# First two image pairs convolved from the colour planes, with warm-up products on TensorE

## The reference

```python
w = (0.2989, 0.587, 0.114)
gray = jnp.einsum('bchw,c->bhw', x, w)[:, None]
edges = conv_general_dilated(gray, scharr, window_strides=(1, 1), padding='SAME', ...)
h = jnp.sqrt(jnp.square(edges)).sum(axis=1) / 2
...
k, v, r = (einsum('btc,dc->btd', mix(layernorm(h)), W) for W in (Wk, Wv, Wr))
h = h + einsum('btc,dc->btd', sigmoid(r) * wkv(w, u, k, v), Wo)   # wkv: a scan over 256 tokens
h = h + experts(layernorm(h))    # one of 8 experts per token: gelu((xhat*s+b) @ W1 + b1) @ W2 + b2
```

## Time and profile before

| what | us |
|---|---|
| median of 3 runs | 1179.91 (1176.8 to 1180.4) |
| the profiled execution | 1180.26 |
| its span, first to last instruction | 1178.5 |
| PE busy | 1097.7 (93%) |
| DVE busy | 1033.9 (88%) |
| ACT busy | 880.0 (75%) |
| POOL busy | 171.4 (15%) |

### The profile page before, as it was taken

The page is one execution under the profiler, slowest core; times in us unless marked ns, Lnnn a source line. Parts: engine busy times, 40 slices in busy tenths (PEclk is TensorE's granted clock), DMA queues, the critical chain, the costliest instruction groups (busy, mean ns, idle before and its releaser), DMA issues.

```text
span 1178.5 us, 17076 instructions
## 1 busy us (share of the span) xinstructions
PE 1097.7 (93%) x5699; PEld 715.6 (61%) x5699; DVE 1033.9 (88%) x1869; ACT 880.0 (75%) x1407; POOL 171.4 (15%) x234
## 2 busy tenths in 40 slices
PE   0647899999999999999999999999999999999987
PEld 0223466666666666666666666666666666666665
DVE  2587799999999999999999999999999999999851
ACT  0366687888788878878888878888888788877641
POOL 4021110101111101011111111111111111110000
PEclk9878899999999999999999999999999999999999
DMA  7986667667766776677767676677676766760001
GB/s 190 204 161 110 103 149 158 141 123 153 152 140 135 156 153 146 123 141 155 144 136 146 154 153 134 124 163 148 131 147 146 163 136 123 152 99 22 19 18 36
DMA packets 163601, 155.70 MB, mean 132 GB/s; under 512 B 12444, under 2 KB 163570, under 8 KB 163570
## 3 DMA queue, kind: packets, MB, share of 16 engines
q1 hardware_dynamic: 125972, 119.77, 41.4%
q0 software_dynamic: 32640, 31.46, 21.6%
q10 hardware_dynamic: 4958, 4.07, 1.5%
HBM read 105.96 MB, written 65.03 MB: 145 GB/s over the span
## 4 chain that ended last, share of the span: by engine, by line
PE 88%; DMA 6%; SPq 2%; ACT 1%; DVE 1%; POOL 0%; issue 0%; ACTq 0%; POOLq 0%
PE bank L1135 26%; PE bank L1270 19%; PE bank L1198 15%; PE bank L1125 10%; PE bank L1174 9%; PE bank L1219 4%; DMA gray_dram<-planes 2%; DMA gray_dram<-rows_in 2%; DMA rows_in<-gray_dram 2%; PE bank L1248 2%; PE bank L1271 1%; PE bank L1210 1%; PE bank L1257 1%; SPq L346 1%; PE bank L1186 1%; DMA gray_dram<-in_x_dram 1%
## 5 line engine op out<-in xcount | busy, mean ns | idle before, releaser
L1270 PE MATMUL bank<-w_sb,hidden 128*128 128x256 f32 x1024 | 238.8, 380 | 1.9 <-ACT hidden L963 1.9
L1270 PEld LDWEIGHTS bank<-w_sb,hidden 128*128 128x128 f32 x1024 | 184.8, 191 | 30.1 <-ACT hidden L963 2.6
L1125 PE MATMUL bank<-rows_in,conv_w 102*32 102x512 f32 x1024 | 138.3, 641 | 47.9 <-DMA rows_in<-gray_dram 47.9
L1135 PE MATMUL bank<-mixed_r,w_r_t 128*128 128x512 f32 x256 | 127.4, 622 | 8.8 <-ACT v_sb L892 8.8
L1198 PE MATMUL bank<-normed_hi,w_hi 128*128 128x512 f32 x256 | 128.2, 501 | 3.2 <-DVE normed_lo L721 3.2
L1135 PE MATMUL bank<-mixed_v,w_v_t 128*128 128x512 f32 x256 | 122.0, 600 | 0.4 <-ACT edge L876 0.4
L1174 PE MATMUL bank<-w_o_t,rwkv 128*128 128x256 f32 x512 | 116.9, 382 | 0.3 <-DVE rwkv L695 0.3
L440 POOL TENSOR_TENSOR pool_turn<-pool_turn 128x1 f32<-128x1 f32 x30 | 5.5, 184 | 721.8 <-ACT planes L884 676.3
L1174 PEld LDWEIGHTS bank<-w_o_t,rwkv 128*128 128x128 f32 x512 | 98.2, 192 | 15.7 <-issue 1.1
L1198 PE MATMUL bank<-normed_lo,w_hi 128*128 128x512 f32 x256 | 101.4, 396 | 0.0
L1198 PE MATMUL bank<-normed_hi,w_lo 128*128 128x512 f32 x256 | 100.8, 394 | 0.0
(11 more groups left out here) (144 smaller groups left out, 2308.3 us busy)
## 6 DMA issues: line engine op xcount, KB each, us to landing
rows_in<-gray_dram SPq DMA_DIRECT2D x186, 256.0 KB
planes<-in_x_dram SPq DMA_DIRECT2D x124, 256.0 KB, 3.5
gray_dram<-planes POOLq DMA_DIRECT2D x120, 256.0 KB, 5.9
out_dram<-resid SPq DMA_DIRECT2D x64, 256.0 KB, 2.2
gray_dram<-in_x_dram SPq DMA_DIRECT2D x60, 256.0 KB, 5.1
rows_in<-gray_dram SPq DMA_DIRECT2D x124, 24.0 KB
rows_in<-gray_dram ACTq DMA_DIRECT2D x6, 256.0 KB
planes<-in_x_dram ACTq DMA_DIRECT2D x4, 256.0 KB, 7.3
```

What stands on the lines that cost most here:

```text
L1125: ins = pe.matmul(bank[BANK_EDGE[n]][ROW_TILE * q:ROW_TILE * (q + 1), :], conv_w[0:TAPS, c, :], rows, start=True, stop=True)
L1135: ins = pe.matmul(ps[:, :], weights[:, kt, ct * P:(ct + 1) * P], part[:, 2 * kt:2 * kt + 2, :].rearrange("p i t -> p (i t)"), start=(kt == ...
L1270: pe.matmul(ps, hidden[:, m, i, rows], w2_sb[:, m, :], start=(m == 0), stop=False)
```

## The change

- The first two pairs no longer go through gray. `load_colors` brings, for each pair, the red, green and blue rows straight from `x` into `rows_in`: the three groups of 32 partitions now hold the three colours, unshifted, and the six extra partitions the rows above and below in each colour (zeroed by DVE where there are none). SP and ACT take one image each, first the first pair, then the second.
- `convolve` does three accumulating products for such a pair where there was one: a centre one of 512 columns and two of 2 x 255 columns, displaced by one to the right or left in the result. Their weights `color_w` are built by DVE from the taps, the filter and the gray weights (`shade`).
- PE first runs `WARM_UP = 12` products of a cleared tile of 128 x 512 in fp32, as soon as DVE has cleared it.
- ACT's list has the filter's 18 numbers first, then the rows, then the parameters and Wr, and last the shifted filter taps and the zero borders of `gray_dram`, now written as two strips of lines and 4 x 257 pairs of elements.
- SP's `load_later_weights` stands before step 3 instead of step 2. DVE's `conv_w` and `ident_bf` are built in `setup_first_layer`, before step 3. POOL builds taps first, then the identity; the mask and the clearing of `b2_raw` come last.

The core of the diff:

```diff
+        def load_colors(eng, pair, i):
+
+            buf, base = pair % 2, (2 * pair + i) * NCOL * T * D
+            for color in range(NCOL):
+                src = bass.AP(x.tensor, base + color * T * D, [[D, ROW_TILE], [ROW_TILE * D, TILES], [1, D]])
+                eng.dma_start(rows_in[buf][ROW_TILE * color:ROW_TILE * (color + 1), :, i, :], src
+                              ).then_inc(rows_loaded[buf], 16)
+            if pair < 2:
+                eng.wait_ge(s_outside, 2 * pair + 2)
+            for k in range(2):
+                src = bass.AP(x.tensor, base + (ROW_TILE - 1 + k) * D,
+                              [[T * D, NCOL], [ROW_TILE * D, TILES - 1], [1, D]])
+                first = 3 * ROW_TILE + 3 * k
+                eng.dma_start(rows_in[buf][first:first + 3, 1 - k:TILES - k, i, :], src
+                              ).then_inc(rows_loaded[buf], 16)
...
-            load_first(sp, 0, 0)
-            load_first(sp, 1, 0)
-            store_first(sp, 0, 0)
-            sp.wait_ge(s_borders, 16)
-            sp.wait_ge(first_stored[0], 16 * HALF)
-            load_rows(sp, 0, 0)
-            store_first(sp, 1, 0)
+            load_colors(sp, 0, 0)
+            load_colors(sp, 1, 0)
             for src, dst in zip((Wk, Wv), w_raw):
                 sp.dma_start(dst, src.rearrange("(a p) c -> p a c", p=P)).then_inc(s_w_in, 16)
-            sp.wait_ge(first_stored[1], 16 * HALF)
-            load_rows(sp, 1, 0)
...
+                    if at.is_step(FIRST + GRAY):
+                        sp.wait_ge(s_borders, 32)
...
-            run_steps(sp, step, {2: load_later_weights})
+            run_steps(sp, step, {3: load_later_weights})
...
-            first_gray_of(0)
-            dve.wait_ge(s_scharr_dj_in, 80)
+            for b in range(2):
+                dve.memset(rows_in[b][3 * ROW_TILE:TAPS, 0, :, :], 0.0).then_inc(s_outside, 1)
+                dve.memset(rows_in[b][3 * ROW_TILE:TAPS, TILES - 1, :, :], 0.0).then_inc(s_outside, 1)
+            dve.memset(zeros, 0.0).then_inc(s_zeros, 1)
+            for color in range(NCOL):
+                dve.memset(shade[ROW_TILE * color:ROW_TILE * (color + 1), :], GRAY_WEIGHTS[color])
+            for n in range(6):
+                dve.memset(shade[3 * ROW_TILE:TAPS - n, :], GRAY_WEIGHTS[2 - n % 3]).then_inc(s_shade, 1)
+                dve.wait_ge(s_shade, n + 1)
+
+            dve.wait_ge(s_scharr_all_in, 16)
+            done(dve.tensor_scalar(scharr_all[0:TAPS, :], scharr_all[0:TAPS, :], shade[0:TAPS, :], 0.5,
+                                   ALU.mult, ALU.mult))
             dve.wait_ge(s_cleared, CLEARED_TAPS)
+            for di in range(3):
+                for c in range(2):
+                    weights = scharr_all[0:TAPS, 9 * c + 3 * di:9 * c + 3 * di + 3]
+                    ins = dve.tensor_tensor((color_w if di == 0 else color_part)[0:TAPS, c, :, :],
+                                            taps[0:TAPS, di, :].unsqueeze(1).to_broadcast([TAPS, 3, ROW_TILE]),
+                                            weights.unsqueeze(2).to_broadcast([TAPS, 3, ROW_TILE]), ALU.mult)
+                if di > 0:
+                    ins.then_inc(s_color_part, 1)
+                    dve.wait_ge(s_color_part, di)
+                    done(dve.tensor_tensor(color_w[0:TAPS, :, :, :], color_w[0:TAPS, :, :, :],
+                                           color_part[0:TAPS, :, :, :], ALU.add))
...
             def setup_first_layer():
+                setup_conv()
                 dve.wait_ge(s_w1_in, 32)
...
+            act.wait_ge(s_zeros, 1)
+            act.dma_start(bass.AP(gray_dram.tensor, 0, [[IMAGE, 4], [(T + 1) * PITCH + 1, 2], [1, T + 1]]),
+                          zero_pairs[:, 0:T + 1].unsqueeze(1).to_broadcast([4, 2, T + 1])).then_inc(s_borders, 16)
+            act.dma_start(bass.AP(gray_dram.tensor, D + 1, [[IMAGE, 4], [PITCH, T + 1], [1, 2]]),
+                          zero_pairs.rearrange("p (t k) -> p t k", k=2),
+                          allow_slow_non_contiguous=True).then_inc(s_borders, 16)
...
-            pe.wait_ge(s_dve_setup, SETUP_CONV)
+            pe.wait_ge(s_zeros, 1)
+            for _ in range(WARM_UP):
+                pe.matmul(bank[BANK_Y[1]][:, :], zeros[:, 0:P], zeros[:, 0:512], start=True, stop=True)
+            pe.wait_ge(s_dve_setup, SETUP_FIRST)
...
+                rows = rows_in[at.buf(EDGE)][0:TAPS, 4 * half:4 * half + 4, :, :]
+                if at.has_later(EDGE):
...
+                else:
+                    sums = pair_view(bank[BANK_EDGE[n]])
+                    for dj, to, of in ((1, 0, 0), (0, 1, 0), (2, 0, 1)):
+                        width = D - (dj != 1)
+                        for q in range(4):
+                            ins = pe.matmul(sums[ROW_TILE * q:ROW_TILE * (q + 1), :, to:to + width],
+                                            color_w[0:TAPS, c, dj, :], rows[:, q, :, of:of + width],
+                                            start=(dj == 1), stop=(dj == 2))
```

More of the change, by code:

```diff
@@ L190, in vision_layer @@
         w1_scaled = resid[0][:, :, :].rearrange("p (a b) d -> p a (b d)", a=CH)
[L191 to L195, removed]
+        late_flat = resid[3][:, :, :].rearrange("p b d -> p (b d)")
+        color_w = late_flat[:, 0:6 * ROW_TILE].rearrange("p (c j r) -> p c j r", c=2, j=3)
+        color_part = late_flat[:, 6 * ROW_TILE:12 * ROW_TILE].rearrange("p (c j r) -> p c j r", c=2, j=3)
+        scharr_all = late_flat[:, 12 * ROW_TILE:12 * ROW_TILE + 18]
+        shade = late_flat[:, 12 * ROW_TILE + 18:12 * ROW_TILE + 19]
+        zeros = resid[2][:, :, :].rearrange("p b d -> p (b d)")[:, 0:2 * (T + 1)]
+        zero_pairs = zeros[0:4, :]
         w1_raw = hidden[:, 0:2, :, :].rearrange("p a b c -> p a (b c)")
@@ L210, in vision_layer @@
         planes_in = [sem(f"planes_in{i}") for i in range(2)]
[L211 to L214, removed]
+        s_outside, s_shade, s_zeros, s_scharr_all_in = [sem(n) for n in ("outside", "shade", "zeros", "scharr_all_in")]
+        s_color_part = sem("color_part")
         s_params_in, s_scharr_dj_in, s_borders = sem("params_in"), sem("scharr_dj_in"), sem("borders")
@@ L427, in _ @@
             pool.memset(eps[:, 0:1], LN_EPS)
-            pool.memset(eps[:, 1:2], LN_EPS * LN_EPS)
+            pool.memset(eps[:, 1:2], LN_EPS * LN_EPS).then_inc(s_built, 1)
+            pool.memset(b2_raw, 0.0).then_inc(s_cleared, 1)
+            pool.memset(mask_rows[:, :], MASK_OUT).then_inc(s_cleared, 1)
+            pool.wait_ge(s_cleared, CLEARED_B2 + 1)
+            for g in range(NM):
+                rows = slice(32 * g, 32 * (g + 1))
+                pool.affine_select(out=mask_rows[rows, :], in_=mask_rows[rows, :], compare_op=ALU.is_ge, fill=0.0,
+                                   base=0, pattern=[[1, E * H]], channel_multiplier=-H).then_inc(s_cleared, 1)
+                pool.wait_ge(s_cleared, CLEARED_B2 + 2 + 2 * g)
+                pool.affine_select(out=mask_rows[rows, :], in_=mask_rows[rows, :], compare_op=ALU.is_ge, fill=0.0,
+                                   base=H - 1, pattern=[[-1, E * H]], channel_multiplier=H).then_inc(s_cleared, 1)
+                pool.wait_ge(s_cleared, CLEARED_B2 + 3 + 2 * g)
+            pool.tensor_scalar(mask_rows[:, :], mask_rows[:, :], -1.0, MASK_OUT, ALU.mult, ALU.add
+                               ).then_inc(s_cleared, 1)
             pool.memset(b2_parts[:, :], 0.0)
             pool.memset(wg_t[:, :, :], 0.0)
-            pool.memset(route[:, :, :], 0.0).then_inc(s_built, 1)
+            pool.memset(route[:, :, :], 0.0).then_inc(s_cleared, 1)
             def step(at):
@@ L492, in _ @@
-                done(ins)
-            first_gray_of(1)
-            dve.wait_ge(s_built, 1)
-            done(dve.tensor_copy(ident_bf[:, :], ident[:, :]))
-            assert own[0] == SETUP_CONV
+                    weights = scharr_all[0:TAPS, 9 * c + 3 * di:9 * c + 3 * di + 3]
+                    ins = dve.tensor_tensor((color_w if di == 0 else color_part)[0:TAPS, c, :, :],
+                                            taps[0:TAPS, di, :].unsqueeze(1).to_broadcast([TAPS, 3, ROW_TILE]),
+                                            weights.unsqueeze(2).to_broadcast([TAPS, 3, ROW_TILE]), ALU.mult)
@@ new lines, in _, with setup_conv @@
+                if di > 0:
[3 more added lines that the diff above has]
+                                           color_part[0:TAPS, :, :, :], ALU.add))
+            assert own[0] == SETUP_FIRST
+            def setup_conv():
+                dve.wait_ge(s_scharr_dj_in, 80)
+                done(dve.tensor_scalar(scharr_dj[0:TAPS, :], scharr_dj[0:TAPS, :], 0.5 * GRAY_WEIGHTS[2], None,
+                                       ALU.mult))
+                for di in range(3):
+                    for c in range(2):
+                        weight = scharr_dj[0:TAPS, 3 * c + di:3 * c + di + 1]
+                        if di == 0:
```

(9 more changed lines are left out.)

129 lines of the change are left out of this document (37 added, 92 removed).

## The result

The changed kernel takes 1165.95 us in the median of its runs against 1180.16 of the kernel before beside it; the ratio is 0.988, with a 95% interval of 0.985 to 0.991. The forecast for the time was 1165.3 us. The profiled execution was the longest of the four, at 1167.08 us; its span, from the first to the last instruction, is 1165.3 us and only by chance the same number as the forecast.

What follows compares the result with a forecast made beforehand. PE bounds the loop, so time is the third convolution's start plus 1089.5 us. C at 26.9, scaling's end 46.3 and 28.1 more put that start at 74.4 instead of 89.03: forecast 1165.3 us, range 1160 to 1175.

Steps and rivals of the forecast that it cites:

- The sum: Start of the kernel: added-up terms put the third pair's convolution at 74.4 us, 14.6 earlier than 89.03.
- zeros: PE's start: twelve fp32 products of zeros take 24 x 0.43 + 2.5 = 12.8 us, ending at 16.6.
- first convolution: First pair on PE: 24 groups of 0.43 us make 10.3 us, or 20.5 if the level does not hold.
- C: End of the first pair's convolution: forecast at 26.9 us, 13.1 earlier than the 39.96 before.
- its first two results: Second pair's convolution: 12 groups instead of 4, 12 x 0.43 + 2.5 = 7.7 us, reaching 43.7.
- from there to the third: End of scaling to third convolution: the old 29.1 us stretch stays, less 1.0 for a POOL operation, giving 28.1.
- the POOL operation of 2.06 us: One-element operation at 67.15 before the third convolution: beside a DVE scan, perhaps not in the new order; 1.0 taken off.
- the rival with 0.12: Rows late, chance 0.12: both pairs share the queues, first pair lands at 20 to 22, 4 to 5 us lost, 1170.
- The clock rival: Chance 0.12: zeros may not raise PE's level, or narrow products lose it; C 37.1, gain 4.4, kernel 1175.5 us.
- the planes' early arrival: Step 3: third pair's plane loads, now ahead of the weights, are long in, so scaling ends at 46.3 us.
- The rival with 0.06: ACT held, chance 0.06: short descriptors hold ACT until 37, C counts as 39, gain about 2, kernel 1177.9 us.
- The slack before the first scan of step 4: DVE's idle time there: 5.69 - 4 - 1.6 leaves 0.1 us, so DVE's later work is just hidden.

Runs made afterwards that it cites:

- e2: Changed kernel with 20 products of zeros instead of 12; ratio to the kernel before 0.9952, third convolution 6.0 us later than in the first trace.
- e1: Changed kernel without the products of zeros (WARM_UP = 0); ratio to the kernel before 0.9901, third convolution at 76.27 us.
- e7: Changed kernel without zeros, SP and ACT holding the second pair's row loads until the first pair's rows landed; ratio to the kernel before 0.9879.
- e5: Changed kernel with only the centre product for the first two pairs, so edges differ from the reference; one execution, span 1158.1 us, third convolution 68.27.
- e3: Changed kernel with the experts' weights issued before step 2 on SP again, ahead of the third pair's planes; ratio to the kernel before 0.9888.
- e10b: As e8, but Wk, Wv, parameters and Wr loaded before the second pair's rows, and nine products of zeros; ratio to the kernel before 0.9891.
- e6: Changed kernel with ACT's scaling of the third pair moved ahead of absolute(0) and absolute(1) in step 3; ratio to the kernel before 0.9883.
- e11b: As e10b, with scharr_dj loaded right behind the first pair's rows and setup_conv() called before step 0; ratio to the kernel before 0.9857, median 1162.85 us.
- e8: Changed kernel with the edits of e6 and e7 together and seven products of zeros; ratio to the kernel before 0.9878, median 1162.4 us.
- e4: Kernel before with only the experts' weights moved on SP, issued before step 3 instead of step 2; ratio to the kernel before 0.9997.
- e9b: The changed kernel measured and traced again, unchanged (the repeat); ratio to the kernel before 0.9891, median 1165.51 us.

## Why the prediction was right

**The third convolution.** The sum said 74.4; the trace says 74.35 and, again, 74.40. Its terms, in us:

| term | forecast | first trace | repeat |
|---|---|---|---|
| start of PE | 3.8 | 3.80 | 3.81 |
| zeros | 12.8 | 13.26 | 12.50 |
| first convolution | 10.3 | 10.46 | 10.46 |
| its end, C | 26.9 | 27.5 | 26.8 |
| C to the second convolution | 9.07 | 8.9 | 8.9 |
| its first two results | 7.7 | 7.14 | 8.45 |
| end of scaling | 46.3 | 46.05 | 46.6 |
| from there to the third | 28.1 | 28.3 | 27.8 |

The mechanism is the one forecast, and every term is within 0.8 us. That the sum is right to 0.05 us is luck, for the misses cancel. The start of PE is exact because a memset takes 0.48 to 0.49 us and not 0.6, while the first starts at 0.99 and not at 0.8. In the last stretch the POOL operation of 2.06 us came back almost whole (0.19 at 54.03), where I had taken off 1.0; but from the end of the scaling to the red add it now takes 1.9 us (0.45 of them the operation at 46.20), and had taken 1.1 from the landing of blue.

**That C is on the path** is shown by e2: 6.7 us more in front became 6.0 at the third convolution, and the time rose with it.

**The rows.** I took their landing at 14.5; it is 15.5 (e1). The zeros end 1.5 us later, 0.8 in the repeat, so the miss cost nothing. That the second pair in the queue delays the first, the rival with 0.12, is true, with 2.4 us (e7), and the range of 20 to 22 that I gave it was too dark.

**The zeros.** The sum took them as given and did not price the kernel without them. They are worth 1.9 us of the 14.7 at the third convolution (e1). The rest is by subtraction the new way of the rows, net of the 6.1 us that the tripling costs (e5); no run takes that way back alone. The clock rival did not come: with zero products PE's level rose after 4 to 5.5 us, and in the narrow products that followed it stayed (groups 0.43 us apart up to 26.44). In the sum, 24 x 0.43 + 2.5 = 12.8, the 0.43 is the distance of the zeros' weight loads from 9.61 on (before, mixed_v's eight instructions took 3.60), and for the 2.5 of a start at the low level the two traces show 3.0 and 2.2 (13.26 and 12.50 less 10.3).

**The order on SP.** The prediction gave the planes' early arrival as the reason why scaling would not wait. The planes are early, but e3 shows that they would have been in time in the old order too. The step was right in its sum and wrong in the weight it gave the move.

**ACT.** I put it free at 20 to 24; it was at 22.4 with its table loaded, 5 us before it was needed at C. The rival with 0.06 did not come here, but e10b shows it at work: there ACT issues until 25.5 and turns to the last of the four results only at 28.4, 3.7 us after PE had finished it.

**DVE.** The slack before the first scan of step 4 was 0.1 us by the sum; it is 1.51 in the first trace and nothing in the repeat, in e1 and in e3. So the forecast was right that DVE is just hidden, and the path from the second convolution over PE, ACT and DVE is by now as long as the one over the transfers: e6 shortens the second by 3.9 us, and the fourth convolution gains 0.8. The prediction listed the 1.8 us of DVE's added setup among what eats this slack; e11b, set beside e10b, shows that they lie in a wait for PE and cost nothing.

**After the third.** The fourth convolution was forecast 34.9 after the third; 35.98 and 34.42 were measured. The profiled execution was forecast at 1165.6 and took 1167.08, and 1.1 of the 1.5 us are this round. A difference of under 1.6 us at the fourth convolution is therefore nothing that one pair of traces can show.

## What to carry to other kernels

Where the loop is bound by one engine, take the start as a path of its own, find the first moment from which that engine never waits, and price a change only at that moment. Work tripled on an engine that idles behind transfers can be cheaper than the round trip it saves. After each wait that is removed the next one stands within a few microseconds (here rows, weights behind them, ACT's issuing, and then the second convolution's own way over PE, ACT and DVE), so look at the two or three runners-up before moving one. Products of zeros ahead of the data were worth 1.9 us here, less than the 2.2 to 3.0 us by which they ran longer while the clock was still low (12.50 and 13.26 against 24 x 0.43 = 10.3): weigh them by what they save, and end them when the data are there. And take a second trace before building on a first: the long round and DVE's idle time were one execution's own, e8's span was the shortest of six, and e10b's forecast was built on it.

## What the runs showed of the hardware

A row load to 32 partitions, alone and with all DMA engines busy, moved 200 to 247 GB/s where a load to 128 moved 343 (e7); its last four us ran at 169 down to 4 GB/s. The same adding DMA to DRAM took 5.95 us before, 5.93 in the changed kernel and 9.37 in e4, where 2 MB of other loads were issued within three us of its start. With products of zeros PE's weight loads went from 0.86 to 0.43 us apart after 5.5 us in the first trace and 4 in e9b. With products of data it took 6.4 us in e1 and, in the trace of before, 4.0 (from 49.03 to 53.0), about 5 (from 68.56 to 73.5) and 7.4 (from 123.90 to 131.3) until the level was up. How long ACT was held in issuing changed with the order of its small transfers: in e10b it issued until 25.5, and with the five loads of scharr_dj moved ahead (e11b) until 19.3.
